# TensorE clears the banks of the sums, and ScalarE fetches a row set in every fourth round

## The chip, the core and the metric

The kernel runs on one core of one Trainium2 chip. Five engines work side by side: TensorE (PE, with its weight loads PEld), VectorE (DVE), ScalarE (ACT), GpSimd (POOL) and SyncE (SP). Each works through its own list of instructions in order and waits on semaphores that others raise. The metric is the device time of one execution in microseconds; less is better.

## The reference

One layer of a graph network with typed edges, then a GRU cell, a residual and a layer norm. There are 12500 nodes of 128 values and 212500 edges, sorted by their target node:

```
all_msgs = einsum('nh,thd->ntd', h, message_W) + message_b        # 8 types
messages = segment_sum(all_msgs[src, edge_type], dst, num_segments=12500)
gi = messages @ gru_w_ih.T + gru_b_ih ;  gh = h @ gru_w_hh.T + gru_b_hh
r = sigmoid(i_r + h_r) ; z = sigmoid(i_z + h_z) ; n = tanh(i_n + r * h_n)
out = layernorm(x + (1 - z) * n + z * h)
```

## The kernel before, in words

The kernel sums rows first and applies the type weights to the sums. The edges lie in tiles of 128, each edge of a tile on a partition. The source rows of a tile are gathered from HBM (128 rows of 512 bytes) by one indirect DMA that GpSimd issues. A product of those rows with a one-hot matrix (made by VectorE) adds them, by target node and type, into one of three PSUM banks `agg[0..2]` ("the sums' banks").

The work goes in 98 rounds, one per tile of 128 nodes. Rounds 0 to 10 ("early") have 17 edge tiles, rounds 11 to 97 ("packed") have 16, in groups c = 0, 1, 2 of 6, 5 and 5 tiles, one bank per group. Round 97 is the last, and has one tile more. In a packed round r:

- GpSimd gathers the 16 tiles of round r into `rows` or `rows_other`, in turn. Before it starts on group c it waits until TensorE has used that group two rounds earlier (`tiles_done`), so it may run nearly two rounds ahead.
- TensorE (`packed_round`) counts, sums group 0, applies the type weights to the sums of round r-1 (`apply_weights`), sums groups 1 and 2, spreads a row of counts of self-loops (`spread_loops`, which needs ScalarE's `copy_loops`), and makes the GRU gates of node tile r-2.
- ScalarE (`packed_round`) does, in this order: the sigmoids of node tile r-3 (`finish_rz`, line 834), a copy, the tanh (`finish_n`, line 842), then `fetch_rows(r, 0)`; then, when group 0 is summed and the weights are applied, it copies `x_turned`, `counts` and `loop_row`, copies bank 0 to SBUF and overwrites the bank with zeros (`copy_sums`, `zero_sums`), the same for bank 1, copies `loops`, does `fetch_rows(r, 1)`, and at last copies and clears bank 2. All these copies stand under line 726.
- VectorE (`packed_round`): one-hot matrices of groups 1 and 2, then `finish(r-3)` (gate arithmetic and layer norm, begun by `t_rh`, line 1238, which needs the sigmoids), masks and a one-hot for round r+1, `add_messages`, `add_loops` (lines 1177 and 1181, which end in the row `work<-work,loop_counts`, and which `copy_loops` on ScalarE waits for), `make_messages`, `loop_x`.

So there is a ring between two engines: sigmoids of round r, VectorE's `finish` to `add_loops`, ScalarE's `copy_loops`, its second batch of `fetch_rows`, its copy of bank 2, and the sigmoids of round r+1.

`fetch_rows` takes one edge tile in six rounds off GpSimd: ScalarE reads row numbers into registers (`TENSOR_LOAD`, line 892) and issues one 512-byte DMA per row (line 896), 16 ahead of the waits of the round and 8 behind `copy_loops`, until 128 rows stand in a spare slot of `rows`. The tile is used as the last of group 2 in rounds 17, 23, ..., 95 (`FETCH_ROUNDS`, 14 of them), where GpSimd gathers 15 tiles in place of 16. SyncE brings the row numbers (`load_fetch_index`).

Of the kernel before, what the change touches and what calls it, by code (L numbers as in the profile page):

```python
# [16 lines left out]
def gnn_kernel(nc, x, src, dst, etype, w_msg, b_msg, w_ih, w_hh, b_ih, b_hh, out):  # L17
# [51 lines left out]
    FETCH_SLOT = (ROUND - 1) % ROW_TILES  # L69
    FETCH_STEP = FETCH_EVERY * ROUND // ROW_TILES  # L70
    FETCH_TILE = GROUPS[2] - 1
    assert FETCH_EVERY * ROUND % ROW_TILES == 0 and (FETCH_EVERY - 1) * (FETCH_AHEAD + FETCH_BEHIND) + FETCH_BEHIND == P
    REACH = (P + SPAN + SAMPLE) // SAMPLE
# [33 lines left out]
    with ctx:  # L107
# [113 lines left out]

        fetch_src = w_ih_rows[:, 0, :].bitcast(I32)
        fetch_index = bias_part[0][0:1, :].bitcast(I32).rearrange("o (s e) -> o s e", e=P)
# [113 lines left out]
        tiles_done = [sem(f"tiles_done{c}") for c in range(3)]  # L337
        sums_read = [sem(f"sums_read{c}") for c in range(3)]
        sums_copied = [sem(f"sums_copied{c}") for c in range(3)]
# [149 lines left out]
        def _(sp):  # L489
# [69 lines left out]
            def load_fetch_index(m):  # L559
                row = (m + 1) * FETCH_STEP + 1  # L560
                sp.dma_start(fetch_index[0:1, m % 2, :], fetch_src[row:row + 1, :]).then_inc(fetch_index_in[m % 2], 16)

# [6 lines left out]
            with sp.If(flag):  # L569
# [25 lines left out]
                for r in range(EARLY + 1, LAST):  # L595
                    round_(r)
                    m = (r - EARLY) // FETCH_EVERY + 1
# [126 lines left out]
        def _(act):  # L724
# [119 lines left out]
            def fields_as_floats(r):  # L844

                for n, name in ((0, "src"), (2, "type"), (3, "next_kind")):
                    act.wait_ge(packing, AT[name])
                    copy(part(n).bitcast(F32)[:, 0:ROW_SLOTS], part(n)[:, 0:ROW_SLOTS]).then_inc(fields_ready, 1)
                    if n == 0:
                        act.wait_ge(fields_ready, 1)  # L850
                        copy(fetch_src[0:ROWS, :], src_words[:, FETCH_SLOT * P:(FETCH_SLOT + 1) * P]).then_inc(fetch_src_ready, 1)

# [30 lines left out]
            def fetch_rows(r, behind):  # L883

                m, step = divmod(r - EARLY - 1, FETCH_EVERY)
                if m >= len(FETCH_ROUNDS) or behind and fetches(r):
                    return
                a = step * (FETCH_AHEAD + FETCH_BEHIND) + behind * FETCH_AHEAD
                n = min(FETCH_BEHIND if behind else FETCH_AHEAD, P - a)
                if step == 0 and not behind:  # L890
                    act.wait_ge(fetch_index_in[m % 2], (m // 2 + 1) * 16)
                _, numbers = nc.values_load_multi_w_load_instructions(
                    fetch_index[0:1, m % 2, a:a + n], engines=[act.engine], min_val=0, max_val=NODES - 1,
                    skip_runtime_bounds_check_because="row numbers, as the gathers take them")
# [659 lines left out]
        def _(pe):  # L1554
# [78 lines left out]
            def sum_tiles(r, c, offs):  # L1633
                _, n, start = groups(r)[c]
                if r > 0:
                    pe.wait_ge(sums_copied[c], r)
                pe.wait_ge(onehot_ready[c], r + 1)
                ahead = isinstance(r, int) and r in (1, 2)
# [5 lines left out]
                for k in range(n):  # L1644
                    if r == LAST:
                        pe.wait_ge(gathered_last[start + k], 16)
                    slot = start + k
                    if fetches(r) and c == 2 and k == FETCH_TILE:
                        m, slot = (r - EARLY) // FETCH_EVERY - 1, SPARE_SLOT
                        pe.wait_ge(fetched[m % 2], (m // 2 + 1) * P * 16)  # L1650
                    last = nc.tensor.matmul(agg[c][:, ds(offs[c][k] * TYPES, CODES)],  # L1651
                                            place[:, slot, :],
                                            onehot[c][:, k, :], start=False, stop=True, skip_group_check=True)
# [235 lines left out]
```

## Time and profile before

| | us |
|---|---|
| three runs | 1990.95, 1994.47, 1996.48 (median 1994.47) |
| the profiled execution, its own time | 1993.74 |
| its span, first to last instruction | 1991.6 |
| mean granted TensorE clock | 0.843 of full speed |

An engine's busy time counts instructions that compute or gather. Issuing a DMA, loading registers and waiting are not counted, so ScalarE's share does not hold the 1792 DMAs of `fetch_rows`. In a timeline, `ACT` rows are computing instructions, `ACTq` rows are DMA issues; the bracket at the end gives the idle time before the row and what ended it. For ScalarE that idle time holds DMA issues too.

### The profile page before, as it was taken

What the parts mean: (1) busy time and instruction counts of PE and PEld (TensorE: products, weight loads), DVE (VectorE), ACT (ScalarE), POOL (GpSimd) and SP (SyncE); (2) the same over time, 40 slices, a digit from 0 to 9 for tenths busy, and PEclk for the clock granted to TensorE, in tenths of its full rate; (3) what the DMA queues carried; (4) which work ended last, traced back from release to release, by engine and by line L of the source; (5) the groups of instructions that cost most, each with busy time, mean ns of one, the idle gap of its engine ahead of it and who ended that gap; (6) DMA issues with size and microseconds to landing.
All of it is one profiled execution on the core that took longest, in us unless ns stands there. A gap on an engine that the chain in (4) does not pass through costs nothing.

```text
span 1991.6 us, 34610 instructions
## 1 busy us (share of the span) xinstructions
PE 1372.3 (69%) x6657; PEld 1045.8 (53%) x6657; DVE 1245.0 (63%) x4650; ACT 595.0 (30%) x1489; POOL 1488.7 (75%) x1578
## 2 busy tenths in 40 slices
PE   1766676767676767676767777767676766766676
PEld 1755555555555555455545555545455555555554
DVE  7887465656565656565656566656565656565566
ACT  2323423232323232323232323232222323232222
POOL 7777777777777777777777777777777777777774
PEclk9877878888888888787878888888888888888889
DMA  5222222222222222222222222222222222222221
GB/s 128 58 62 64 56 64 65 66 62 64 63 66 61 65 63 65 62 65 62 66 61 66 63 65 63 64 63 65 63 64 63 64 63 63 63 65 63 64 63 45
DMA packets 100626, 128.44 MB, mean 64 GB/s; under 512 B 33280, under 2 KB 74959, under 8 KB 100478
## 3 DMA queue, kind: packets, MB, share of 16 engines
q0 software_dynamic: 50112, 102.73, 19.8%
q1 hardware_dynamic: 46584, 23.07, 4.2%
q10 hardware_dynamic: 3782, 0.93, 0.2%
q8 instruction: 61, 1.00, 0.2%
q14 instruction: 87, 0.71, 0.1%
HBM read 120.16 MB, written 6.40 MB: 64 GB/s over the span
## 4 chain that ended last, share of the span: by engine, by line
POOL 65%; issue 22%; DVE 8%; PE 3%; ACT 1%; DMA 1%; DVEq 0%; SPq 0%; ACTq 0%; POOLq 0%
POOL rows_other L660 33%; POOL rows L660 32%; DVE work L1317 1%; DVE codes L1314 1%; PE agg L1651 1%; DVE onehot L1150 1%; PE msg L1678 1%; DMA work<-in_src_dram 0%; DVE root_a L1224 0%; DVE messages_T L1166 0%; ACT sums_room L726 0%; ACT agg L726 0%; DVEq L1157 0%; PE gates L1717 0%; PE turn L1733 0%
## 5 line engine op out<-in xcount | busy, mean ns | idle before, releaser
L660 POOL DMA_INDIRECT rows<-in_x_dram,src_T x843 | 801.2, 950 | 260.9 <-issue 256.1
L660 POOL DMA_INDIRECT rows_other<-in_x_dram,src_T x688 | 651.8, 947 | 209.8 <-issue 209.8
L1651 PE MATMUL agg<-onehot,rows 128*128 128x128 f32 x1714 | 288.0, 330 | 256.9 <-DMA rows<-in_x_dram,src_T 255.9
L1678 PE MATMUL msg<-sums_room,w_type 128*128 128x320 f32 (+1 forms) x1552 | 443.1, 442 | 13.8 <-issue 10.3
L1651 PE MATMUL agg<-onehot,rows_other 128*128 128x128 f32 x1376 | 232.7, 330 | 259.6 <-DMA rows_other<-in_x_dram,src_T 258.3
L1651 PEld LDWEIGHTS agg<-onehot,rows 128*128 128x128 f32 x1714 | 259.6, 236 | 277.6 <-issue 276.6
L1678 PEld LDWEIGHTS msg<-sums_room,w_type 128*128 128x128 f32 x1552 | 306.2, 205 | 122.3 <-issue 27.0
L1199 DVE SCALAR_TENSOR_TENSOR sums_room<-turn,x_turned 128x128 f32<-128x128 f32 x696 | 145.6, 281 | 350.7 <-PE turn L1697 350.7
L1651 PEld LDWEIGHTS agg<-onehot,rows_other 128*128 128x128 f32 x1376 | 208.2, 235 | 278.5 <-issue 278.5
L726 ACT ACTIVATE sums_room<-agg 128x512 f32<-128x512 f32 x293 | 173.3, 591 | 375.7 <-PE agg L1651 327.6
L1150 DVE TENSOR_TENSOR onehot<-code_T,codes 128x640 f32<-128x640 f32 (+1 forms) x294 | 244.3, 859 | 18.9 <-PE agg L1651 18.8
L726 ACT ACTIVATE x_turned<-cnt 128x128 f32<-128x128 f32 x97 | 26.9, 277 | 670.9 <-PE msg L1680 573.9
L726 ACT ACTIVATE agg<-zeros_f 128x512 f32<-128x512 f32 x294 | 176.6, 601 | 9.4
L1138 DVE TENSOR_TENSOR node_mask<-rel_T,codes 128x320 bf16<-128x320 f32 (+3 forms) x294 | 139.1, 473 | 0.0
L1712 PE MATMUL gates<-w_hh_T,x_T 128*128 128x384 f32 x194 | 126.8, 751 | 0.0
L1166 DVE TENSOR_TENSOR messages_T<-messages_T,msg 128x64 f32 x291 | 63.9, 219 | 79.3 <-PE msg L1680 46.8
L1717 PE MATMUL gates<-w_ih_T,messages 128*128 128x384 f32 x194 | 107.5, 646 | 1.9 <-DVE messages L1207 1.9
L1177 DVE TENSOR_TENSOR loop_counts<-counts,loop_row 1x192 f32<-1x192 f32 x87 | 30.4, 350 | 97.1 <-ACT loop_row L726 87.6
L1616 PEld LDWEIGHTS cnt<-node_mask,type_mask 128*128 128x128 bf16 (+1 forms) x783 | 64.4, 105 | 47.6 <-issue 24.7
L1616 PE MATMUL cnt<-node_mask,type_mask 128*128 128x128 bf16 (+1 forms) x783 | 86.9, 228 | 0.0
L1717 PEld LDWEIGHTS gates<-w_ih_T,messages 128*128 128x128 f32 x194 | 54.5, 282 | 51.4 <-issue 42.8
L1181 DVE TENSOR_TENSOR work<-work,loop_counts 1x64 f32 x261 | 56.4, 216 | 37.3 <-DVE loop_counts L1177 0.2
(219 smaller groups left out, 1357.0 us busy)
## 6 DMA issues: line engine op xcount, KB each, us to landing
rows<-in_x_dram ACTq DMA_DIRECT2D x1792, 0.5 KB
rows<-in_x_dram,src_T POOLq DMA_INDIRECT x843, 2.5
rows_other<-in_x_dram,src_T POOLq DMA_INDIRECT x688
x_next<-in_x_dram SPq DMA_DIRECT2D x97, 64.0 KB
out_dram<-out_tile SPq DMA_DIRECT2D x97, 64.0 KB
x_tile<-in_x_dram SPq DMA_DIRECT2D x96, 64.0 KB
work<-in_dst_dram SPq DMA_DIRECT2D x1, 609.4 KB
work<-in_src_dram SPq DMA_DIRECT2D x1, 609.4 KB
```

The lines of the kernel that those rows point to most:

```text
L660: nc.gpsimd.indirect_dma_start(out=to, out_offset=None, in_=x[:, :], in_offset=bass.IndirectOffsetOnAxis(ap=index, axis=0),).then_inc(done ...
L726: return nc.scalar.activation(to, value, ACT.Copy)
L1138: nc.vector.tensor_tensor(node_mask[c][:, 0:n, 0:wide], rel_T[:, cols].unsqueeze(2).broadcast_to([P, n, wide]), codes[:, 0:wide].unsqueeze ...
L1150: nc.vector.tensor_tensor(onehot[c][:, 0:n, :], code_T[:, ds(column(r, start), n)].unsqueeze(2).broadcast_to([P, n, CODES]), codes[:, 0:CO ...
L1166: ins = nc.vector.tensor_tensor(messages_T[:, ds(node, WINDOW)], messages_T[:, ds(node, WINDOW)], bank[:, c * WINDOW:(c + 1) * WINDOW], AL ...
L1181: ins = nc.vector.tensor_tensor(loops_T[:, ds(node, WINDOW)], loops_T[:, ds(node, WINDOW)], (loop_counts if since(r, EARLY) else counts)[0 ...
L1199: done = nc.vector.scalar_tensor_tensor(out=to[:, t, :], in0=turn[:, 0:P], scalar=t - NO_LOOP, in1=values, op0=ALU.is_equal, op1=ALU.mult)
L1616: last = nc.tensor.matmul(cnt[0:m * HALF, c * P:c * P + m * WINDOW], type_mask[c][:, k:k + m, :].rearrange("p k t -> p (k t)"), node_mask[ ...
L1651: last = nc.tensor.matmul(agg[c][:, ds(offs[c][k] * TYPES, CODES)], place[:, slot, :], onehot[c][:, k, :], start=False, stop=True, skip_gr ...
L1678: nc.tensor.matmul(msg[:, 0:cols], w_type[:, t, :], sums[:, t, 0:cols], start=t == 0, stop=False, skip_group_check=True)
L1712: nc.tensor.matmul(bank[:, HID:4 * HID], x_lhs, w_hh_T[:, :], start=False, stop=False)
L1717: nc.tensor.matmul(gates_of(j)[:, 0:GATE], value, w_ih_T[:, :], start=False, stop=True).then_inc(gates_ready, 1)
```

## The change

- `zero_sums` is gone from ScalarE. `copy_sums` raises `sums_copied` by itself. TensorE, in `sum_tiles`, waits for it and clears the bank with a product of zeros (one row of 128 weights by 512 columns, bf16) before it waits for the one-hot and for the gathered rows. This holds for each group of rounds 1 to 97.
- A tile is fetched in every fourth round, in rounds 16, 20, ..., 96 (21 tiles). ScalarE issues 16 row DMAs ahead and 16 behind in each of the rounds 12 to 95, 32 in place of 24 (or 8 in a round that uses a fetched tile).
- The fetched rows land in two places in turn: the spare slot of `rows`, and `w_hh_rows`, whose content is no longer needed.
- The row numbers come from three places of a row of edges and not one; a copy in round 8 is wider for that.

```diff
-    FETCH_EVERY = 6
-    FETCH_AHEAD, FETCH_BEHIND = 16, 8
-    FETCH_ROUNDS = tuple(range(EARLY + FETCH_EVERY, LAST, FETCH_EVERY))
+    FETCH_EVERY = 4
+    FETCH_LOT = 16
+    FETCH_ROUNDS = tuple(range(EARLY + 1 + FETCH_EVERY, LAST, FETCH_EVERY))
+        fetch_rooms = (rows[:, SPARE_SLOT, :], w_hh_rows[:, 0, :])
...
                 read = copy(to, agg[c][:, :].rearrange("p (n t) -> p t n", t=TYPES))
-                if isinstance(r, int) and r == LAST:
-                    read.then_inc(sums_copied[c], 1)
-                else:
-                    read.then_inc(sums_read[c], 1)
-                    act.wait_ge(sums_read[c], r + 1)
-                    zero_sums(c).then_inc(sums_copied[c], 1)
+                read.then_inc(sums_copied[c], 1)
...
                 m, step = divmod(r - EARLY - 1, FETCH_EVERY)
-                if m >= len(FETCH_ROUNDS) or behind and fetches(r):
+                if m >= len(FETCH_ROUNDS):
                     return
-                a = step * (FETCH_AHEAD + FETCH_BEHIND) + behind * FETCH_AHEAD
-                n = min(FETCH_BEHIND if behind else FETCH_AHEAD, P - a)
-                if step == 0 and not behind:
+                a = (2 * step + behind) * FETCH_LOT
+                if a == 0:
                     act.wait_ge(fetch_index_in[m % 2], (m // 2 + 1) * 16)
...
                 for p, number in enumerate(numbers, a):
-                    act.dma_start(rows[p:p + 1, SPARE_SLOT, :], x[ds(number, 1), :]).then_inc(fetched[m % 2], 16)
+                    act.dma_start(fetch_rooms[m % 2][p:p + 1, :], x[ds(number, 1), :]).then_inc(fetched[m % 2], 16)
...
                 if r > 0:
                     pe.wait_ge(sums_copied[c], r)
+                    nc.tensor.matmul(agg[c][:, :], zeros_b[0:1, 0:P], zeros_b[0:1, 0:512], start=True, stop=True)
                 pe.wait_ge(onehot_ready[c], r + 1)
```

The order on ScalarE in the middle of a packed round, before (`x_turned` to the first DMA of the batch behind; an `ISA` row and a `DMA` row together are one fetched row, and 8 such pairs follow in all):

```order
L726 ACTIVATE x_turned<-cnt 128x128
L726 ACTIVATE counts<-cnt 64x192 x2
L726 ACTIVATE loop_row<-cnt 1x192
L726 ACTIVATE sums_room<-agg0 128x8x64
L726 ACTIVATE agg0<-zeros_f 128x512
L726 ACTIVATE sums_room<-agg1 128x8x64
L726 ACTIVATE agg1<-zeros_f 128x512
L726 ACTIVATE loops<-work 1x128
L892 TENSOR_LOAD bias_part0
L896 ISA
L896 DMA rows<-in_x_dram 1x128
```

The same place in the changed kernel, where 16 pairs follow:

```order
L729 ACTIVATE x_turned<-cnt 128x128
L729 ACTIVATE counts<-cnt 64x192 x2
L729 ACTIVATE loop_row<-cnt 1x192
L729 ACTIVATE sums_room<-agg0 128x8x64
L729 ACTIVATE sums_room<-agg1 128x8x64
L729 ACTIVATE loops<-work 1x128
L887 TENSOR_LOAD bias_part0
L891 ISA
L891 DMA w_hh_rows<-in_x_dram 1x128
```

Two clears are gone ahead of `loops`, one more goes behind the copy of bank 2, and the batch between `loops` and that copy is twice as long.

The order on TensorE from the type weights to group 1, before:

```order
L1678 MATMUL msg<-sums_room,w_type 128x320 x8
L1680 MATMUL msg<-counts,b_type 128x192
L1651 MATMUL agg1<-onehot1,rows_other 128x128
L1651 ISA
L1651 MATMUL agg1<-onehot1,rows_other 128x128
```

And in the changed kernel:

```order
L1675 MATMUL msg<-sums_room,w_type 128x320 x8
L1677 MATMUL msg<-counts,b_type 128x192
L1632 MATMUL agg1<-zeros_f 128x512
L1648 MATMUL agg1<-onehot1,rows_other 128x128
L1648 ISA
```

One product of zeros stands ahead of each group, three in a round.

## Rows read from the trace of the kernel before

**Rows 1.** The page's busy time of each engine.
```profile
PE 1372.3 (69%) x6657; PEld 1045.8 (53%) x6657; DVE 1245.0 (63%) x4650; ACT 595.0 (30%) x1489; POOL 1488.7 (75%) x1578
```

**Rows 2.** The page's chain that ended last, by engine.
```profile
POOL 65%; issue 22%; DVE 8%; PE 3%; ACT 1%; DMA 1%; DVEq 0%; SPq 0%; ACTq 0%; POOLq 0%
```

**Rows 3.** Timeline of POOL: start us, us, what; near 1009 us and at the end.
```profile
1008.82 0.95 POOL L660 DMA_INDIRECT rows<-in_x_dram,src_T  x1 [0.30 <-issue]
...
1970.41 0.94 POOL L660 DMA_INDIRECT rows<-in_x_dram,src_T  x1 [0.30 <-issue]
```

**Rows 4.** Timeline of PE in a middle round and near the end.
```profile
1007.94 1.58 PE L1651 MATMUL agg<-onehot,rows 128*128 128x128 f32 x12 [1.93 <-DMA rows<-in_x_dram,src_T]
...
1020.17 2.47 PE L1651 MATMUL agg<-onehot,rows 128*128 128x128 f32 x10 [4.77 <-DMA rows<-in_x_dram,src_T]
...
1953.18 0.28 PE L1697 MATMUL turn<-loops,spread 1*128 1x128 bf16 x1
```

**Rows 5.** Timeline of ACT in a middle round.
```profile
1002.86 0.60 ACT L726 ACTIVATE sums_room<-agg 128x512 f32<-128x512 f32 x1 [4.84 <-PE agg L1651]
...
1005.15 0.26 ACT L834 ACTIVATE gates<-gates 128x128 f32<-128x128 f32 x1 [1.06 <-PE gates L1717]
...
1006.76 0.28 ACT L842 ACTIVATE gates<-t_pre 128x128 f32<-128x128 f32 x1 [0.97 <-DVE t_pre L1240]
1008.12 5.99 ACTq L896 DMA_DIRECT2D rows<-in_x_dram  x16
1014.37 0.28 ACT L726 ACTIVATE x_turned<-cnt 128x128 f32<-128x128 f32 x1 [7.32 <-PE msg L1680]
...
1016.18 0.60 ACT L726 ACTIVATE agg<-zeros_f 128x512 f32<-128x512 f32 x1
1016.72 0.58 ACT L726 ACTIVATE sums_room<-agg 128x512 f32<-128x512 f32 x1
...
1017.86 0.30 ACT L726 ACTIVATE loops<-work 1x128 bf16<-1x128 bf16 x1
1018.74 3.03 ACTq L896 DMA_DIRECT2D rows<-in_x_dram  x8
1022.73 0.60 ACT L726 ACTIVATE sums_room<-agg 128x512 f32<-128x512 f32 x1 [4.57 <-PE agg L1651]
```

**Rows 6.** ACT by line, 280 to 1925 us: busy and mean, idle before, releaser.
```profile
L834 ACT ACTIVATE gates<-gates 128x128 f32<-128x128 f32 x83 | 21.6, 260 | 108.4 <-PE gates L1717 108.2
```

**Rows 7.** Timeline of ACT in round 12.
```profile
275.36 0.26 ACT L834 ACTIVATE gates<-gates 128x128 f32<-128x128 f32 x1 [0.27 <-PE gates L1717]
...
287.75 0.29 ACT L726 ACTIVATE loops<-work 1x128 bf16<-1x128 bf16 x1
288.42 3.03 ACTq L896 DMA_DIRECT2D rows<-in_x_dram  x8
291.57 0.60 ACT L726 ACTIVATE sums_room<-agg 128x512 f32<-128x512 f32 x1 [3.53 <-issue]
...
292.74 0.23 ACT L834 ACTIVATE gates<-gates 128x128 f32<-128x128 f32 x1
```

**Rows 8.** Timeline of DVE in round 12, and in the middle round.
```profile
275.84 0.29 DVE L1238 TENSOR_TENSOR t_rh<-rz,gates 128x128 f32<-128x128 f32 x1
...
286.58 0.92 DVE L1181 TENSOR_TENSOR work<-work,loop_counts 1x64 f32 x3 [0.23 <-DVE loop_counts L1177]
...
1016.84 0.98 DVE L1181 TENSOR_TENSOR work<-work,loop_counts 1x64 f32 x3
```

**Rows 9.** The load of row numbers (line 892): duration in ns, least, median, most.
```profile
L892 ACTq TENSOR_LOAD <-bias_part x154: 713/725/1204, 276.5 to 1920.1; - x154
```

**Rows 10.** Timeline of ACT: the sigmoids of rounds 96 and 97.
```profile
1936.61 0.26 ACT L834 ACTIVATE gates<-gates 128x128 f32<-128x128 f32 x1 [1.43 <-PE gates L1717]
...
1956.54 0.26 ACT L834 ACTIVATE gates<-gates 128x128 f32<-128x128 f32 x1 [1.97 <-PE gates L1717]
```

**Rows 11.** Line 1709: TensorE's products of 128 x 512 in bf16, ns.
```profile
L1709 PE MATMUL gates<-bias_parts,rows x97: 379/606/634, 74.5 to 1975.9; 128*128 128x512 bf16 x97
```

More of the change, by code:

```diff
@@ L65, in gnn_kernel @@
     SAMPLE = 16
-    FETCH_EVERY = 6
-    FETCH_AHEAD, FETCH_BEHIND = 16, 8
-    FETCH_ROUNDS = tuple(range(EARLY + FETCH_EVERY, LAST, FETCH_EVERY))
-    FETCH_SLOT = (ROUND - 1) % ROW_TILES
-    FETCH_STEP = FETCH_EVERY * ROUND // ROW_TILES
+    FETCH_EVERY = 4
+    FETCH_LOT = 16
+    FETCH_ROUNDS = tuple(range(EARLY + 1 + FETCH_EVERY, LAST, FETCH_EVERY))
+    FETCH_PLACES = tuple(divmod((r - EARLY) * ROUND + ROUND - 1, ROW_TILES) for r in FETCH_ROUNDS)
+    FETCH_SLOTS = 3
     FETCH_TILE = GROUPS[2] - 1
-    assert FETCH_EVERY * ROUND % ROW_TILES == 0 and (FETCH_EVERY - 1) * (FETCH_AHEAD + FETCH_BEHIND) + FETCH_BEHIND == P
+    FETCH_FIRST = min(slot for _, slot in FETCH_PLACES)
+    assert FETCH_EVERY * 2 * FETCH_LOT == P
+    assert all((slot - FETCH_FIRST) % FETCH_EVERY == 0 for _, slot in FETCH_PLACES) and FETCH_SLOTS * FETCH_EVERY == ROW_TILES
     REACH = (P + SPAN + SAMPLE) // SAMPLE
@@ L195, in gnn_kernel @@
         zeros_f = sb("zeros_f", [P, 512])
+        zeros_b = zeros_f[:, :].bitcast(BF16)
         messages_T = sb("messages_T", [P, ACC_ROWS])
@@ L219, in gnn_kernel @@
         assert TYPES * END_COLS + P + HID <= (EARLY + 4) * P
-        fetch_src = w_ih_rows[:, 0, :].bitcast(I32)
+        fetch_src = w_ih_rows[:, :, :].rearrange("p a e -> p (a e)").bitcast(I32).rearrange("p (a e) -> p a e", e=P)
+        fetch_rooms = (rows[:, SPARE_SLOT, :], w_hh_rows[:, 0, :])
         fetch_index = bias_part[0][0:1, :].bitcast(I32).rearrange("o (s e) -> o s e", e=P)
@@ L337, in gnn_kernel @@
         tiles_done = [sem(f"tiles_done{c}") for c in range(3)]
-        sums_read = [sem(f"sums_read{c}") for c in range(3)]
         sums_copied = [sem(f"sums_copied{c}") for c in range(3)]
@@ L559, in load_fetch_index @@
             def load_fetch_index(m):
-                row = (m + 1) * FETCH_STEP + 1
-                sp.dma_start(fetch_index[0:1, m % 2, :], fetch_src[row:row + 1, :]).then_inc(fetch_index_in[m % 2], 16)
+                row, slot = FETCH_PLACES[m]
+                sp.dma_start(fetch_index[0:1, m % 2, :], fetch_src[row:row + 1, (slot - FETCH_FIRST) // FETCH_EVERY, :]).then_inc(fetch_index_in[m % 2], 16)
             def round_(r):
@@ L596, in _ @@
                     round_(r)
-                    m = (r - EARLY) // FETCH_EVERY + 1
+                    m = (r - EARLY - 2) // FETCH_EVERY + 1
                     if fetches(r - 1) and m < len(FETCH_ROUNDS):
@@ L764, in _ @@
             copy(w_hh_T[:, :], msg[:, 0:GATE]).then_inc(turned_copied, 1)
-            def zero_sums(c):
-                return copy(agg[c][:, :], zeros_f[:, :])
             def zero_counts():
@@ L850, in fields_as_floats @@
                         act.wait_ge(fields_ready, 1)
-                        copy(fetch_src[0:ROWS, :], src_words[:, FETCH_SLOT * P:(FETCH_SLOT + 1) * P]).then_inc(fetch_src_ready, 1)
+                        slots = src_words[:, 0:ROW_SLOTS].rearrange("r (a k e) -> r a k e", k=FETCH_EVERY, e=P)
+                        copy(fetch_src[0:ROWS, :, :], slots[:, :, FETCH_FIRST, :]).then_inc(fetch_src_ready, 1)
             def copy_field(n):
@@ L885, in fetch_rows @@
                 m, step = divmod(r - EARLY - 1, FETCH_EVERY)
-                if m >= len(FETCH_ROUNDS) or behind and fetches(r):
+                if m >= len(FETCH_ROUNDS):
                     return
-                a = step * (FETCH_AHEAD + FETCH_BEHIND) + behind * FETCH_AHEAD
-                n = min(FETCH_BEHIND if behind else FETCH_AHEAD, P - a)
-                if step == 0 and not behind:
+                a = (2 * step + behind) * FETCH_LOT
+                if a == 0:
                     act.wait_ge(fetch_index_in[m % 2], (m // 2 + 1) * 16)
                 _, numbers = nc.values_load_multi_w_load_instructions(
-                    fetch_index[0:1, m % 2, a:a + n], engines=[act.engine], min_val=0, max_val=NODES - 1,
+                    fetch_index[0:1, m % 2, a:a + FETCH_LOT], engines=[act.engine], min_val=0, max_val=NODES - 1,
                     skip_runtime_bounds_check_because="row numbers, as the gathers take them")
                 for p, number in enumerate(numbers, a):
-                    act.dma_start(rows[p:p + 1, SPARE_SLOT, :], x[ds(number, 1), :]).then_inc(fetched[m % 2], 16)
+                    act.dma_start(fetch_rooms[m % 2][p:p + 1, :], x[ds(number, 1), :]).then_inc(fetched[m % 2], 16)
             def packed_round(r):
@@ L1646, in sum_tiles @@
                         pe.wait_ge(gathered_last[start + k], 16)
-                    slot = start + k
+                    tile_rows = place[:, start + k, :]
                     if fetches(r) and c == 2 and k == FETCH_TILE:
-                        m, slot = (r - EARLY) // FETCH_EVERY - 1, SPARE_SLOT
+                        m = (r - EARLY - 1) // FETCH_EVERY - 1
+                        tile_rows = fetch_rooms[m % 2]
                         pe.wait_ge(fetched[m % 2], (m // 2 + 1) * P * 16)
                     last = nc.tensor.matmul(agg[c][:, ds(offs[c][k] * TYPES, CODES)],
-                                            place[:, slot, :],
+                                            tile_rows,
                                             onehot[c][:, k, :], start=False, stop=True, skip_group_check=True)
```

## The prediction

> **What bounds the kernel now.** I read the busy shares first: POOL has the most, 75%, and ACT only 30% [rows 1]. The chain that ended last is POOL for 65% and "issue" for 22%, which together is nearly all of the span [rows 2]. The POOL timeline shows why: each gather takes 0.95 us and 0.30 us of issue lies before it, so one starts every 1.25 us, from the start to 1970.41 [rows 3]. TensorE waits for the gathers, 1.93 us before group 0 and 4.77 us before group 2 of a round [rows 4]. So by the page, GpSimd is the bound, and a gather taken from it is worth 1.25 us.
>
> The second reading is ScalarE's timeline, since its 30% leaves out the DMA issues [rows 5]. In the middle round, which lasts 19.87 us (1002.86 to 1022.73), 16 row DMAs take 5.99 us and 8 take 3.03, so 0.37 us for each one after the first, and ScalarE can do nothing else meanwhile. What is free is 1.06 us before the sigmoids, 0.97 before the tanh and 0.96 before the copy of bank 2 (1021.77, where the batch ends, to 1022.73). The mean wait at the sigmoids is 108.4 / 83 = 1.3 us [rows 6]. That is the slack of the ring that runs through ScalarE and VectorE.
>
> **How fast the ring is when nothing else holds it.** The trace shows this once: in round 12, after a late start, the sigmoids begin at 275.36 and the next at 292.74, 17.38 us later, with 24 DMAs between [rows 7]. GpSimd's pace is 20.0 us for 16 gathers, so the ring had over 2 us to spare. I take it apart:
>
> - Sigmoids to VectorE's last `add_loops`: 275.36 to 287.50 (286.58 + 0.92) is 12.14 us [rows 7, 8]. VectorE started on `t_rh` 0.48 us after the sigmoids and was never idle for long.
> - From there to the first DMA of the batch behind: 288.42 - 287.50 = 0.92. In the middle round it is 1018.74 - 1017.82 = 0.92 too [rows 5, 8], although the copy of `loops` starts 0.25 us after VectorE's end in one and 0.04 in the other. So the loading of row numbers hangs on VectorE's end.
> - The batch of 8: 3.03. To the copy of bank 2: 0.12. That copy with its clear to the next sigmoids: 1.17.
> - Sum 12.14 + 0.92 + 3.03 + 0.12 + 1.17 = 17.38.
>
> **The change part by part.**
>
> *Seven gathers fewer.* 21 fetched tiles for 14: 7 x 1.25 = 8.75 us off GpSimd. A round then has 15.75 gathers in the mean, 19.7 us.
>
> *Three clears off ScalarE.* The two ahead of `loops` (0.60 each, 1016.18 for one) give the ring nothing: what comes next waits for VectorE at 1017.82, and VectorE's work between the sigmoids and that point is untouched. The third, behind the copy of bank 2, is on the ring: 1.17 becomes 0.54, the pitch from such an operation to the next (1016.18 to 1016.72). In the early rounds, where ScalarE and TensorE answer each other, the clears may give up to 1 us once; I take 0.
>
> *Eight more DMAs behind `loops`.* 3.03 becomes 5.99, as in the batch ahead. The load of 16 numbers takes 1.20 us against 0.72 for 8 [rows 9]; the batch ahead shows it too, 1006.76 to 1008.12 is 1.36 where 8 numbers need 0.88 (1017.86 to 1018.74). So 0.92 becomes 1.40.
>
> *The ring after:* 12.14 + 1.40 + 5.99 + 0.12 + 0.54 = 20.19 us. From below: a round without the 0.23 us pause in VectorE's row [rows 8], 19.96, say 20.0. From above: a batch of 16 that takes 0.29 us longer, as one batch in four does before, and somewhat more for longer code, 20.35. I take 20.17. That is over the 19.7 that GpSimd needs. **The ring becomes the bound by 0.47 us a round**, in each of the 84 rounds that fetch (12 to 95).
>
> The batch of `fetch_rows` ahead of the waits is not what decides: from the sigmoids to the tanh 1.6 us (of which VectorE's share is less when it is free), 7.35 to the end of the DMAs, 0.26 to `x_turned` at 1014.37 and 1.2 to the end of `loop_row` (the clear at 1016.18 less one copy of 0.6) make 10.4 at most, and VectorE needs that row only 10.64 after the sigmoids (286.58 less the pause of 0.23 and one operation of 0.35, less 275.36).
>
> *Three products of zeros on TensorE.* A 128 x 512 product in bf16 took 0.38 to 0.61 us [rows 11]; three are 1.1 to 1.8 us a round. Two stand ahead of a wait for gathers of 1.93 and 4.77 us, the one of group 1 eats into the second of these [rows 4]. Covered, and more so when the ring is late. If not covered, they would cost GpSimd nothing until TensorE is nearly two rounds behind. At the very end the one for group 2 of round 97 stands on the path: 0.3 us.
>
> *Two places for the rows, index loads, wider copy.* The rows land a round before use, the copy is in round 8 beside waits: 0.
>
> *What waits behind the late ring.* When ScalarE is late, TensorE's `apply_weights` starts late, but it had 4 us before that and 4.8 before group 2. GpSimd's gathers run nearly two rounds ahead and would be held only when the ring is about 30 us late or more (an estimate: gathers for round r+2 begin some 1.7 rounds of 20 us after the sigmoids of round r). So the lateness grows quietly, 0.47 x 84 = 39 us, and is paid at the end.
>
> **The sum.** Rounds 12 to 96 are 84 rings from the sigmoids at 275.36: 275.36 + 84 x 20.17 = 1969.6, where before the same sigmoids stood at 1936.61 [rows 10], held by GpSimd. Round 96 fetches nothing: VectorE 12.1, copy of `loops` 0.3, then from `spread_loops` to the sigmoids 3.4 (1953.18 to 1956.54) [rows 4, 10] make 15.8 in place of 19.93; at full clock it may be 15. I take 15.4: 1985.0. The rest, 1991.6 - 1956.54 = 35.1, is a chain of latencies of the last two node tiles and stays, with 0.3 for the product: span 2020.4. Around the span lie 1993.74 - 1991.6 = 2.1: 2022.5. The rings' own bounds give 84 x (20.0 to 20.35) = 2008 to 2038. Since GpSimd may be caught up with late and the lower bound 20.0 is the sum of undisturbed rows, I name 2020, which is a ring of 20.14. The profiled execution lies 0.7 us below the median of the runs; that is inside their spread.
>
> **Rules of the Trainium skill.** ScalarE's DMA issue is shown above as 0.37 us per row, 5.99 for 16. "DMA: Bandwidth & Descriptors", section "Issuing engines are not separate DMA queues", says that issuing from another engine saves the sequencer's time for it, "which is usually small relative to the DMA itself". Read so, the 896 extra issues are near to free, and the kernel ends where rival 1 does. The trace does not agree for 512-byte rows: 32 issues are 12 us of a 20 us round. Of the number load, "Perfetto Trace Analysis", section "DVE / Act Engine Instruction", says that an instruction that waits is pushed to a wait queue and the sequencer is ready for the next. By that the load could be done before VectorE ends (rival 2). The constant 0.92 us of this trace speaks against it.
>
> **Rivals.**
>
> 1. *GpSimd stays the bound.* The ring turns out at 19.7 or less, and only the seven gathers count: 1993.74 - 8.75 + 0.3 = 1985.3. For it: the page's chain, ScalarE's 30%, 2 us of waits in its round. Against: those waits plus the freed 0.63 are 3.6, but the 0.97 is VectorE's own time and the addition is 3.4. It decides when the ring is under 19.7; at 19.86 the lateness is (19.86 - 19.7) x 84 = 13 us, of which round 96 gives back 4, and gain and loss cancel.
> 2. *The number load starts before VectorE ends*, once ScalarE has two clears fewer ahead of it. The ring loses up to 1.2 us: 19.0, and the time is that of rival 1, 1985. Against: both rounds above.
> 3. *The ring is only just over.* 19.8 to 19.95: lateness 8 to 21 us, less 4, on 1985: 1989 to 2002, no change in the middle.
> 4. *Row DMAs slow the gathers.* At 1008.82, inside a batch, a gather takes 0.95 as elsewhere [rows 3]. 1% on 1558 gathers would be 15 us beside rival 1, 2000. Little speaks for it.
>
> **Chances.** The forecast 0.79, rivals 1 and 2 together 0.12, rival 3 0.07, rival 4 0.02. About 0.3% (6 us) is what a measurement of this kernel tells from no change. Slower: the forecast and some of rivals 3 and 4, 0.82; same 0.06; faster 0.12. The range reaches from rival 3's end, 2001, to a ring of 20.32, 2035; below it lies the 0.12 of rivals 1 and 2 and a little of 3.
>
> **What would show it.** Right: POOL loses its place at the head of the chain that ended last, to ACTq, ACT and DVE; the distance between two rows of the sigmoids is 20.1 in the middle of the run, whatever the number of gathers; their wait for PE gates is gone; the copy of bank 2 comes right behind a batch of 6.0 us; the first DMA of that batch 1.40 us after VectorE's `work` row; GpSimd's gathers keep 1.25 us and end some 30 us earlier against the end of the span than the 21 us of now. Wrong: sigmoids every 19.7 us with waits before them (rival 1), a first DMA under 1 us after VectorE (rival 2), or gathers over 0.95 us (rival 4).

## The result, and the profile after

| | before | changed |
|---|---|---|
| median (runs) | 1994.01 (1990.95 to 1996.48, 4) | 2029.97 (2027.0 to 2030.8, 4) |
| profiled execution, its span | 1993.74, 1991.6 | 2029.68, 2027.7 |
| mean granted clock | 0.843 | 0.853 |

The ratio is 1.018, with a 95% interval of 1.0168 to 1.0193: 1.8% slower. The forecast was 2020 (2001 to 2035).

The page of the changed kernel, busy time of the engines (beside [rows 1]) and the chain that ended last (beside [rows 2]):

```profile
PE 1446.3 (71%) x6852; PEld 1033.3 (51%) x6948; DVE 1248.3 (62%) x4650; ACT 417.7 (21%) x1198; POOL 1483.0 (73%) x1571
```

```profile
DVE 36%; ACTq 23%; issue 19%; DVEq 11%; ACT 6%; PE 3%; DMA 0%; SPq 0%
```

Every engine's share is within 9 points of before, and POOL still has the most. The chain is another one: POOL had 65% of it and is gone; VectorE, ScalarE's issues and ScalarE have taken its place.

ScalarE's timeline in a middle round (start us, us, what; the bracket is the idle time before the row, in which DMA issues are counted as idle), beside [rows 5]:

```profile
1006.11 0.27 ACT L829 ACTIVATE gates<-gates 128x128 f32<-128x128 f32 x1
...
1007.25 0.28 ACT L837 ACTIVATE gates<-t_pre 128x128 f32<-128x128 f32 x1 [0.48 <-DVE t_pre L1235]
1008.61 5.99 ACTq L891 DMA_DIRECT2D w_hh_rows<-in_x_dram  x16
1014.85 0.28 ACT L729 ACTIVATE x_turned<-cnt 128x128 f32<-128x128 f32 x1 [7.32 <-issue]
...
1015.69 0.32 ACT L729 ACTIVATE loop_row<-cnt 1x192 f32<-1x192 f32 x1
...
1018.25 0.31 ACT L729 ACTIVATE loops<-work 1x128 bf16<-1x128 bf16 x1 [1.13 <-DVE work L1176]
1019.61 6.27 ACTq L891 DMA_DIRECT2D w_hh_rows<-in_x_dram  x16
1026.00 0.60 ACT L729 ACTIVATE sums_room<-agg 128x512 f32<-128x512 f32 x1 [7.45 <-issue]
1026.50 0.27 ACT L829 ACTIVATE gates<-gates 128x128 f32<-128x128 f32 x1
```

The copy of bank 2 and the sigmoids follow the batch without a wait; before, they waited for TensorE. VectorE's timeline in the same round, beside [rows 8]:

```profile
1006.61 0.29 DVE L1233 TENSOR_TENSOR t_rh<-rz,gates 128x128 f32<-128x128 f32 x1 [4.86 <-ACT rz L830]
...
1016.76 0.34 DVE L1172 TENSOR_TENSOR loop_counts<-counts,loop_row 1x192 f32<-1x192 f32 x1 [1.12 <-ACT loop_row L729]
1017.25 0.97 DVE L1176 TENSOR_TENSOR work<-work,loop_counts 1x64 f32 x3
```

VectorE now stands idle 4.86 us ahead of `t_rh` and waits for the sigmoids. The bracket of `loop_counts` names ScalarE's `loop_row`, but that row was done at 1016.01, 0.75 us earlier. What fills the 1.12 us is seen in the chain that ended last, whose longest pieces there are (start us, us, what):

```profile
1015.54 0.31 DVEq L1152
1015.99 0.30 DVEq L1152
1016.41 0.30 DVEq L1152
1016.76 0.35 DVE loop_counts L1172
```

Line 1152 is `first_nodes`: VectorE loads three node numbers into registers, which no busy time counts. They lie on the ring, and in the mean of 84 rings the idle time ahead of `loop_counts` is 1.12 us as well. By line, 280 to 1925 us (busy and mean ns, idle before, releaser), beside [rows 6]:

```profile
L1233 DVE TENSOR_TENSOR t_rh<-rz,gates 128x128 f32<-128x128 f32 x81 | 23.3, 288 | 381.1 <-ACT rz L830 381.1
L829 ACT ACTIVATE gates<-gates 128x128 f32<-128x128 f32 x81 | 22.1, 273 | 0.0
```

The sigmoids' 108.4 us of waiting are 0.0, and VectorE's waiting for them is 381.1. GpSimd's timeline in the same round and at the end, beside [rows 3]:

```profile
1006.71 0.94 POOL L663 DMA_INDIRECT rows<-in_x_dram,src_T  x1 [0.30 <-issue]
...
1974.21 0.94 POOL L663 DMA_INDIRECT rows<-in_x_dram,src_T  x1 [0.30 <-issue]
1985.09 0.94 POOL L663 DMA_INDIRECT rows<-in_x_dram,src_T  x1 [9.93 <-PE agg L1648]
```

A gather is as long as before. From 1336 us on GpSimd waits for TensorE once in a while, 23 times and 31.4 us in all, of which 9.93 stand ahead of the very last gather, which waits for TensorE's round 96; the one ahead of that ends 52.6 us before the end of the span, where the last one of before ended 20.2 us before it. The sigmoids of rounds 96 and 97, beside [rows 10]:

```profile
1976.50 0.27 ACT L829 ACTIVATE gates<-gates 128x128 f32<-128x128 f32 x1
...
1992.38 0.26 ACT L829 ACTIVATE gates<-gates 128x128 f32<-128x128 f32 x1 [3.00 <-PE gates L1714]
```

### The profile page after: what moved, and what is told of

Read it like the earlier page. It is cut to its first block, busy times and chain, and to the rows that moved or that the text cites. A ratio compares the mean times of both kernels' runs of the same rounds, so it can differ in the third digit from the quotient of the medians.

```text
span 2027.7 us, 37507 instructions
## 1 busy us (share of the span) xinstructions
PE 1446.3 (71%) x6852; PEld 1033.3 (51%) x6948; DVE 1248.3 (62%) x4650; ACT 417.7 (21%) x1198; POOL 1483.0 (73%) x1571
## 3 DMA queue, kind: packets, MB, share of 16 engines
q10 hardware_dynamic: 5574, 1.39, 0.3%
## 4 chain that ended last, share of the span: by engine, by line
DVE 36%; ACTq 23%; issue 19%; DVEq 11%; ACT 6%; PE 3%; DMA 0%; SPq 0%
ACTq L891 19%; DVEq L1152 8%; ACTq L887 4%; DVE root_a L1219 3%; DVE work L1176 3%; DVE messages_T L1161 3%; DVE rstd L1221 2%; DVE type_mask L1136 2%; DVE loop_counts L1172 2%; DVE stats L1254 1%; DVE t_pre L1235 1%; DVE t_y L1252 1%; DVE gates L1250 1%; DVE t_d L1246 1%; DVE t_zd L1248 1%
## 5 line engine op out<-in xcount | busy, mean ns | idle before, releaser
L663 POOL DMA_INDIRECT rows_other<-in_x_dram,src_T x667 | 631.9, 947 | 207.0 <-issue 197.9
L1233 DVE TENSOR_TENSOR t_rh<-rz,gates 128x128 f32<-128x128 f32 x97 | 27.9, 288 | 408.5 <-ACT rz L830 406.5
L1648 PE MATMUL agg<-onehot,rows 128*128 128x128 f32 x1736 | 264.8, 306 | 11.3 <-DMA rows<-in_x_dram,src_T 11.3
L1694 PE MATMUL turn<-loops,spread 1*128 1x128 bf16 x88 | 23.7, 269 | 347.4 <-ACT loops L729 347.0
L1648 PEld LDWEIGHTS agg<-onehot,rows 128*128 128x128 f32 x1736 | 232.0, 211 | 51.7 <-issue 51.6
L1648 PE MATMUL agg<-onehot,rows_other 128*128 128x128 f32 x1334 | 195.1, 297 | 0.0
L1648 PEld LDWEIGHTS agg<-onehot,rows_other 128*128 128x128 f32 x1334 | 169.6, 203 | 31.6 <-issue 31.6
L1714 PE MATMUL gates<-w_ih_T,messages 128*128 128x384 f32 x194 | 135.6, 800 | 0.9 <-DVE messages L1202 0.9
L1632 PE MATMUL agg<-zeros_f 1*128 1x512 bf16 x291 | 119.3, 410 | 0.0
L1611 PE MATMUL cnt<-node_mask,type_mask 128*128 128x128 bf16 (+1 forms) x783 | 109.0, 269 | 0.0
```

The source lines that it names most:

```text
L663: nc.gpsimd.indirect_dma_start(out=to, out_offset=None, in_=x[:, :], in_offset=bass.IndirectOffsetOnAxis(ap=index, axis=0),).then_inc(done ...
L1611: last = nc.tensor.matmul(cnt[0:m * HALF, c * P:c * P + m * WINDOW], type_mask[c][:, k:k + m, :].rearrange("p k t -> p (k t)"), node_mask[ ...
L1714: nc.tensor.matmul(gates_of(j)[:, 0:GATE], value, w_ih_T[:, :], start=False, stop=True).then_inc(gates_ready, 1)
```

## The experiments

Two theories. *Ring*: the ring of ScalarE and VectorE (sigmoids, `finish` to `add_loops`, `copy_loops`, the batch behind, copy of bank 2, sigmoids) sets the pace, because 8 more row DMAs stand on it. *Rival*: something else does, namely TensorE's products of zeros, the gathers, or the mere total of ScalarE's or a queue's work, wherever it stands.

Twelve kernels ran in four sets. One circumstance has to be known for the numbers: each set ran on a chip of its own, and only the last on one where the kernel before takes 1994 us, as it did above. In the other three it takes 2447 to 2479 us. "Slower chip" below means a chip of these three sets; as each was used in one set only, the runs can't tell a property of the chip from one of the hour. Each kernel is held against the kernel before on its own chip, and each trace is read for its own bounds. Even these ratios carry over only roughly: one and the same program (18 and 14 rows) has 1.077 in one set and 1.089 in another.

| kernel | this | before there | ratio (95%) |
|---|---|---|---|
| e1_clear_only | 2466.1 | 2479.4 | 0.9946 (0.9926 to 0.9965) |
| e2_fetch_only | 2731.9 | 2479.4 | 1.1021 (1.0998 to 1.1043) |
| e3_18_14 | 2668.7 | 2479.4 | 1.0766 (1.0745 to 1.0787) |
| e4_newton1 | 2683.3 | 2479.4 | 1.0822 (1.0800 to 1.0844) |
| f0_changed | 2665.2 | 2446.9 | 1.0899 (1.0870 to 1.0929) |
| f1_clear_only | 2435.5 | 2446.9 | 0.9953 (0.9935 to 0.9970) |
| f3_18_14 | 2660.7 | 2446.9 | 1.0885 (1.0852 to 1.0917) |
| f6_numbers_early | 2646.7 | 2446.9 | 1.0819 (1.0782 to 1.0857) |
| s0_before_const | 2406.7 | 2451.6 | 0.9815 (0.9785 to 0.9846) |
| s1_const | 2425.6 | 2451.6 | 0.9895 (0.9866 to 0.9924) |
| s2_const_18_14 | 2407.8 | 2451.6 | 0.9816 (0.9787 to 0.9846) |
| g0_no_rows | 2010.6 | 1993.8 | 1.0090 (1.0073 to 1.0107) |

### No row DMAs at all (g0_no_rows)

```diff
         def fetches(r):
-            return isinstance(r, int) and r in FETCH_ROUNDS
+            return False
...
-                if m >= len(FETCH_ROUNDS):
+                if True:
                     return
```

> The changed kernel without any row fetched by ScalarE: GpSimd gathers all 16 tiles of every round, and TensorE clears the banks as in the changed kernel. It tells whether ScalarE's row DMAs, and the waits inside them, are what holds the kernels on a chip where the kernel before takes about 2450 us. Theory: without them the ring has 6 us or more to spare and GpSimd bounds at 16 x 1.25 = 20.0 us a round in every round; on such a chip the sigmoids of round 12 stand at 380 us, 84 rounds of 20.0 are 1680, and the end is 50 us behind: 2110 to 2135 us, so GpSimd's 35 gathers more cost nothing against 300 us of the row DMAs. Where the kernel before takes 1994 us: 1985 + 21 x 1.25 = 2011 us. Rival (these chips are slow in other engines as well, the row DMAs are only one part): 2300 us or more.

This is the run that tells the theories apart, and it fell on a chip with the time of the result. It took 2010.6 us against 2011 by the GpSimd sum. GpSimd issues 21 gathers more than in the changed kernel, and the whole is 19 us *faster* than it (ratios to the kernel before 1.009 and 1.018, with intervals that don't touch, and medians of the kernel before that are 0.2 us apart). The page's chain of this kernel:

```profile
POOL 65%; issue 22%; DVE 8%; PE 3%; ACT 1%; DMA 0%; DVEq 0%; SPq 0%; ACTq 0%; POOLq 0%
```

These are the shares of before, to a point. The same two lines as above, 280 to 1925 us:

```profile
L1233 DVE TENSOR_TENSOR t_rh<-rz,gates 128x128 f32<-128x128 f32 x82 | 23.4, 285 | 11.2 <-ACT rz L830 9.8 <-ACT gates L829 1.2
L829 ACT ACTIVATE gates<-gates 128x128 f32<-128x128 f32 x82 | 21.5, 262 | 176.6 <-PE gates L1714 176.6
```

The sigmoids wait 176.6 us for TensorE, and VectorE hardly waits for them: the ring is slack. Its own length without rows can be read in round 12, from ScalarE's timeline:

```profile
277.33 0.26 ACT L829 ACTIVATE gates<-gates 128x128 f32<-128x128 f32 x1 [0.91 <-PE gates L1714]
...
289.54 0.31 ACT L729 ACTIVATE loops<-work 1x128 bf16<-1x128 bf16 x1 [2.43 <-DVE work L1176]
289.75 0.57 ACT L729 ACTIVATE sums_room<-agg 128x512 f32<-128x512 f32 x1
291.77 0.26 ACT L829 ACTIVATE gates<-gates 128x128 f32<-128x128 f32 x1 [1.45 <-PE gates L1714]
```

It is 291.77 - 277.33 = 14.44 us, in which the sigmoids wait 1.45 us for TensorE's gates; the 12.21 from the sigmoids to the copy of `loops` are the changed kernel's 12.14. Put the batch in (from the copy of `loops` to that of bank 2 it takes 7.47 in a round of 5.99 us of DMAs, in place of 0.21) and take off the wait that it covers (from that copy to the sigmoids 0.49 in place of 2.02): 14.44 + 7.26 - 1.53 = 20.17, the changed kernel's ring within 0.1. So the changed kernel passes from GpSimd's bound to the ring's by the row DMAs alone, and products of zeros, which this kernel has too, are not what costs. Before plus 14 gathers of 1.25 us would be 1993.8 + 17.5 = 2011.3; measured are 2010.6, and the interval is some 3 us either way, so nothing that can be told from zero is left for them.

This run takes the rows away altogether, so it does not by itself tell their place from their total. For the place there is the trace of the changed kernel above: the chain that ended last goes through its middle round by VectorE and ScalarE alone, and in that round ScalarE stands idle for 1.13 us ahead of `loops` and waits for VectorE (1.01 in the mean of 84). If ScalarE's total were the bound, it would not.

### The two halves of the change (e1 and f1: clears only; e2: fetching only)

Clears only is the kernel before with this, and without `zero_sums`:

```diff
                     pe.wait_ge(sums_copied[c], r)
+                    nc.tensor.matmul(agg[c][:, :], zeros_b[0:1, 0:P], zeros_b[0:1, 0:512], start=True, stop=True)
```

> The kernel before with one part of the change alone: TensorE clears the banks, ScalarE does not; the fetching stays one tile in six rounds. Theory (the ring through ScalarE and VectorE is what got slow, by the longer batch behind `loops`): the ring here is 17.4 - 0.6 = 16.8 us when free, GpSimd stays the bound, 1991 to 1996 us, no change. Rival (the products of zeros on TensorE cost the time, 291 of 0.41 us = 119 us busy, and an early part that starts the packed rounds 2.8 us later): slower, 2005 us or more.

> The kernel before with the products of zeros on TensorE in place of ScalarE's clears, and the fetching as before. Where the kernel before takes 1994 us, the theory that GpSimd bounds it expects 1991 to 1996 us: the ring gets 0.6 us shorter and has slack anyway, and TensorE's three products are covered by its waits for gathers. If TensorE's products delay the gathers or the start of the packed rounds: 1997 to 2005. Where the ring bounds the kernel before (2479 us), it was 2466.

Fetching only is the changed kernel with ScalarE's clears in place of that product:

> The changed kernel with the clears back on ScalarE: 32 rows fetched a round, no product of zeros. Theory: the ring is 20.22 us as measured plus 0.63 for the one clear that lies on it, 20.85; the two clears ahead of `loops` hide in VectorE's time. 84 rings are 53 us more than in the changed kernel: 2080 us (2070 to 2088). Rival 1 (all three clears are on the ring, 1.8 us): 2180. Rival 2 (the products of zeros are the cost): near the kernel before, 1985 to 1995.

On two chips clears only is 0.5% faster than before, and fetching only, on the first of them, is 10.2% slower. So the loss goes with the fetching and not with the products of zeros; the sizes of the expectations were missed by far, since they were worked out for a chip on which GpSimd bounds the kernel before. Here the clears-only form has a ring of 24.09 us (e1) and 23.74 (f1), where GpSimd needs 20.0 at most, and no GpSimd in the chain that ended last. The kernel before left no trace on such a chip; that it is bound in the same way there is inferred. Fetching only (ring 27.30 us, mean of 84) against the changed kernel (26.55, on another of the slower chips) gives 0.75 us a ring for the clears that are off ScalarE, 0.1 of which may be the chips' (the program with 18 and 14 rows takes 8 us more on the first). The time from the copy of bank 2 to the sigmoids, which I had at 1.17 to 0.54, is 1.16 against 0.49 in the means of these two traces.

### The changed kernel, and rows or work moved within the ring (f0, e3 and f3, f6, e4)

18 rows ahead and 14 behind (e3, f3):

```diff
+    FETCH_AHEAD = 18
-                a = (2 * step + behind) * FETCH_LOT
+                a = 2 * step * FETCH_LOT + behind * FETCH_AHEAD
+                n = 2 * FETCH_LOT - FETCH_AHEAD if behind else FETCH_AHEAD
```

Numbers early (f6) calls `copy_loops(r)` inside `fetch_rows(r, 1)`, between the load of the numbers and the first DMA. e4 leaves out two of the three steps of the root's iteration in layer norm:

```diff
-NEWTON = 3
+NEWTON = 1
```

> The changed kernel itself, as the base that the other kernels of this set are compared with on the same chip. Where the kernel before takes about 1994 us: 2030 us. Where it takes about 2479 us, with gaps in ScalarE's row DMAs, the ring theory expects it well above the kernel before, since 8 more DMAs and a longer load of numbers stand on the ring: the fetch-only kernel took 2732 there, and without its clear on the ring it should be 84 x 0.6 to 84 x 1.2 us less, 2630 to 2690; the rival that GpSimd bounds expects it at or below the kernel before.

> The changed kernel with the 32 rows of a round cut 18 ahead and 14 behind, and not 16 and 16. Theory: behind `loops` the ring loses 2 rows of 0.37 + 0.06 us, 0.86; ahead of it the batch takes 0.86 more, of which VectorE's own 10.64 us hide 0.6. The ring is 19.6, just under GpSimd's 19.7, so GpSimd is the bound again and the seven gathers count: 1985 to 1990 us. Rival (the number of DMAs that ScalarE issues in a round is what costs, wherever they stand): 2030, as the changed kernel.

> The changed kernel with 18 of a round's 32 row DMAs ahead of the waits and 14 behind loops, in place of 16 and 16; nothing else. Ring theory: two DMAs less on the ring are 0.74 us and the shorter load of numbers 0.1, so 20.22 becomes 19.4, GpSimd's 19.7 is the bound again, and the time is 1985 to 1992 us where the changed kernel takes 2030. On a chip where the ring stays the bound, 84 x 0.84 = 70 us less than the changed kernel, more where the DMAs have gaps. Rival (the total of ScalarE's or the queue's work counts, not its place): no change, since 32 DMAs are issued either way. If the batch ahead now ends too late for loop_row, part of the 0.84 is lost: 2000 to 2010.

> The changed kernel with the load of the second batch's 16 row numbers ahead of the copy of loops in place of behind it, so it can be done while ScalarE waits for VectorE. Ring theory: the time from VectorE's last add_loops to the first DMA falls from 1.40 us to about 0.4 (the copy of loops is 0.3), the ring from 20.22 to 19.2 to 19.3, and GpSimd bounds: 1985 to 1992 us. On a chip where the ring stays the bound: 84 x 0.9 = 75 us less than the changed kernel. Rival (the load doesn't lie on the ring, or waits for something else): 2030, no change.

> The changed kernel with 1 step of the root iteration in place of 3, so the norm's root is rough; VectorE's `finish` gets four small operations shorter, about 0.9 us. Theory: VectorE lies on the ring, which becomes 0.6 us shorter (then ScalarE's own batch ahead holds `loop_row`): 19.6, and GpSimd is the bound: 1985 to 1990. Rival (ScalarE alone is full, VectorE is not on the ring): no change, 2030.

The changed kernel came as expected, and none of the others did: f3 gained 4.5 us in place of 70, with runs that overlap those of f0, f6 gained 18.5 in place of 75, and e4 takes 14.6 us longer than e3 in the same set, where both were to end at one time. The reason stands in the traces. ScalarE's timeline of f0_changed:

```profile
1311.38 0.27 ACT L829 ACTIVATE gates<-gates 128x128 f32<-128x128 f32 x1
...
1323.91 0.31 ACT L729 ACTIVATE loops<-work 1x128 bf16<-1x128 bf16 x1 [0.42 <-issue]
1325.26 12.64 ACTq L891 DMA_DIRECT2D rows<-in_x_dram  x16
1338.03 0.60 ACT L729 ACTIVATE sums_room<-agg 128x512 f32<-128x512 f32 x1 [13.81 <-issue]
1338.52 0.27 ACT L829 ACTIVATE gates<-gates 128x128 f32<-128x128 f32 x1
```

The same 16 DMAs take 12.64 us where they took 5.99. Line 891 by operation (duration in ns, least, median, most), first in the kernel of the result, then in f0_changed:

```profile
L891 ACTq FUSED_REGOPS  x2688: 37/37/37, 280.4 to 1975.5; - x192
L891 ACTq DMA_DIRECT2D rows<-in_x_dram x1408: 213/213/490, 280.5 to 1975.7; - x176
```

```profile
L891 ACTq FUSED_REGOPS  x2688: 2/37/730, 380.0 to 2607.4; - x192
L891 ACTq DMA_DIRECT2D rows<-in_x_dram x1408: 3/213/717, 380.2 to 2607.6; - x176
```

The medians are equal. But on this chip there are stretches in which one instruction of ScalarE starts 0.7 us after the other, whatever it does: here an address computation of 37 ns takes up to 730. The mean parts of the 84 rings from the sigmoids of round 12 to those of 96, in us, from these traces:

| | sigmoids to `loops` | `loops` to first DMA | batch behind | to sigmoids | ring |
|---|---|---|---|---|---|
| changed, the result's chip | 12.14 | 1.35 | 6.10 | 0.62 | 20.22 |
| f0_changed | 12.45 | 1.36 | 12.13 | 0.62 | 26.55 |
| f3_18_14 | 13.45 | 3.38 | 9.10 | 0.62 | 26.55 |
| f6_numbers_early | 12.60 | 0.13 | 12.98 | 0.62 | 26.34 |
| e4_newton1 | 12.40 | 1.36 | 12.39 | 0.62 | 26.77 |

What f3 takes from the batch behind comes back in the batch ahead and in the pause before the first DMA; what f6 takes from the load comes back in the batch. And e4 makes VectorE's work shorter (busy 11.3 us a ring for 12.0) without bringing `loops` earlier. In f0, f3, f6 and e4 VectorE's `loop_counts` starts 0.03 to 0.06 us after the end of ScalarE's `loop_row` in the mean, where there are 0.66 on the result's chip: the batch ahead has become part of the ring. So these traces show that ScalarE's own row of instructions bounds the kernel on such a chip. They don't test whether 18 and 14 rows bring it back under GpSimd's pace on the other kind. On this kind the rival "the total counts, not its place" fits f3 (a ring of 26.55 us in both orders).

### Constant row numbers (s0, s1, s2)

One instruction for a DMA in place of three (an address computation, a move, the issue), and half as many DMAs again to keep a batch at 6 us:

```diff
-                    act.dma_start(fetch_rooms[m % 2][p:p + 1, :], x[ds(number, 1), :]).then_inc(fetched[m % 2], 16)
+                    cut = HID // 2 if p % 2 else HID
+                    act.dma_start(fetch_rooms[m % 2][p:p + 1, 0:cut], x[p:p + 1, 0:cut]).then_inc(fetched[m % 2], 16)
+                    if p % 2:
+                        act.dma_start(fetch_rooms[m % 2][p:p + 1, cut:HID], x[p:p + 1, cut:HID]).then_inc(fetched_parts[m % 2], 16)
```

> The kernel before, but its row DMAs read rows with constant numbers (0 to 127), so an issue is one instruction of ScalarE in place of three, and every second row goes as two halves: 24 DMAs ahead and 12 behind in place of 16 and 8; the load of the numbers stays. It leaves out that the rows are the edges' own. Theory of the instruction supply: the stretches of 0.7 us from one instruction of ScalarE to the next come from too many instructions and are gone, the batch of 12 takes about 3 us, GpSimd bounds as it does where the kernel before takes 1994 us, and the time is 1990 to 2010 us. Rival (the DMA queue can't take more rows, so the issues wait): as slow as the kernel before on the same chip, or slower, since there are half as many DMAs again.

> The changed kernel with constant row numbers (0 to 127) and every second row in two halves: 24 DMAs in each batch, one instruction each. It leaves out that the rows are the edges' own. Ring theory: with no stretches of waiting for instructions, sigmoids to the copy of loops 12.1 to 12.5 us, 1.4 to the first DMA, the batch behind B as measured (about 6 us), and 0.6 to the next sigmoids: the ring is 14.2 + B, about 20.2 us, over GpSimd's 19.7, and the time 2015 to 2035 us, slower than the kernel before in the same form. Rival (GpSimd or the total of the DMAs bounds): a ring of 19.7, 1985 to 1992 us. Rival (the queue): as slow as the changed kernel on the same chip or slower.

> As the changed kernel with constant row numbers and halves, but 18 of a round's 32 rows ahead of the waits and 14 behind loops: 27 and 21 DMAs in place of 24 and 24. Ring theory: three DMAs less behind loops are worth 3 x 0.25 us and the load of 14 numbers 0.1, so the ring is 19.4 by itself and GpSimd's 19.7 bounds: 1985 to 1992 us, 30 to 45 us less than with 24 and 24, though the number of DMAs is the same. Rival (the total of ScalarE's work counts, not its place): the same time as with 24 and 24.

The times are 2407 to 2426, not 1990 to 2035: the stretches did not go. The issues in s1_const, the whole rows and first halves:

```profile
L893 ACTq DMA_DIRECT2D rows<-in_x_dram x1408: 3/265/778, 379.4 to 2366.8; - x176
```

ScalarE has 6182 instructions in place of 10384 while half as many DMAs again go to the queue, and the ring is 23.68 us in place of 26.55. That speaks against a queue that can't take more rows. But a batch of 24 behind takes 9.77 us in the mean where the median of the batches ahead is 7.0, so with 40% fewer instructions the stretches are rarer and not gone. What starts one stays open. By its measured parts the ring of s1 is 13.52 + 0.01 + 9.77 + 0.39 = 23.7. It takes 19 us more than s0 on the same chip; the direction is the expected one, at another bound. In s2 the batch behind is down to 6.21 us, yet `loops` comes 17.04 after the sigmoids, since the batch ahead takes 10.94 (the first DMAs of the batch behind start 0.36 us ahead of that copy in the mean): a ring of 17.04 - 0.36 + 6.21 + 0.61 = 23.50, and 18 us less time. As above, such a chip says nothing on GpSimd's bound.

## Why the prediction was right

**The bound changes hands.** As predicted. The ring's mean is (1976.50 - 278.19) / 84 = 20.22 us, GpSimd's pace by its gathers is 15.75 x 1.25 = 19.7, and g0_no_rows shows GpSimd's bound coming back when the row DMAs go.

**The ring's parts.** Medians of those 84 rings but the first: sigmoids to the copy of `loops` 12.14, from there to the first DMA 1.36 (in the middle round 1019.61 - 1018.22 = 1.39 from VectorE's end, forecast 1.40), the batch 5.99, to the copy of bank 2 0.12, to the sigmoids 0.49. The sum is 20.11. I had 20.19 from these parts and went down to 20.14. The mean is over the median because 33 of 83 batches behind take 6.27 us in place of 5.99; "one in four" was too few. My reason for going down, that GpSimd may be caught up with late, was none: the sigmoids never waited.

The 12.14 us of VectorE hold more than the prediction read in them. "Never idle for long" passes over the 1.12 us of register loads ahead of `loop_counts`, in each ring of the kernel before as of the changed one. That the batch ahead is not what decides was right: in the middle round `loop_row` is done 9.90 us after the sigmoids (forecast at most 10.4), and VectorE takes it at 10.65. And the issuing time was set against the length of a round, not against a row's own transfer, of which no view here gives the length.

**The sum, term by term:**

| term | forecast | measured | difference |
|---|---|---|---|
| sigmoids of round 12 | 275.36 | 278.19 | +2.8 |
| 84 rings | 84 x 20.14 = 1691.8 | 1698.3 | +6.5 |
| round 96 | 15.4 | 15.88 | +0.5 |
| tail, with the last product | 35.4 | 35.32 | -0.1 |
| around the span | 2.1 | 1.98 | -0.1 |
| sum | 2020.1 | 2029.7 | +9.6 |

The mechanism was right and two sizes were off. Round 96 was 12.1 + 3.8; the 15.8 worked out from rows was right and the 15.4 that I took was not.

**The clears in the early rounds** I had at 0, with a gain of up to 1 us. The start is 2.8 us later, and in g0_no_rows, which fetches nothing, round 12's sigmoids stand at 277.33, 2.0 later. So, as far as one trace of each can tell, about 2.0 go with the clears on TensorE, and 0.9 are left to the rest. In g0_no_rows it costs nothing at the end, since GpSimd's gathers, which bound it, run a little *ahead* there: its last one starts at 1985.08, and 1970.41 + 14 x 1.25 = 1987.9. In the changed kernel, bound by the ring, it is paid.

**The products of zeros** are covered elsewhere, as predicted. Their line on the page of the changed kernel:

```profile
L1632 PE MATMUL agg<-zeros_f 1*128 1x512 bf16 x291 | 119.3, 410 | 0.0
```

That is 1.2 us a round, in the lower part of the forecast's 1.1 to 1.8, while TensorE waits for `loops` alone 347.0 us in all, 4 us a round:

```profile
L1694 PE MATMUL turn<-loops,spread 1*128 1x128 bf16 x88 | 23.7, 269 | 347.4 <-ACT loops L729 347.0 <-DVE sums_room L1194 0.4
```

**The clear off ScalarE** was priced at 0.63 a ring; on the slower chips 0.67 is read in that place. **GpSimd held late:** its first wait for TensorE in a packed round is at 1336 us, when the ring is some 52 x 0.52 = 27 us behind GpSimd's pace (forecast: about 30). **Rival 2**, the early load of numbers, did not happen: 1.39 us from VectorE's end to the first DMA, none under 1. **Rival 4**: the gathers are 951 and 947 ns in the mean, as before. **Rival 1** (1985) is what the gathers alone would give: 2010.6 - 21 x 1.25 = 1984.4. The 46 us between that and the result are the ring.

**Not settled.** A kernel with a shorter batch behind, or the numbers loaded early, is by the parts above under GpSimd's pace (20.11 less 0.74 and 0.1 is 19.3, and the 0.66 us between `loop_row` and `loop_counts` would take most of the two rows that move there). So, just, is one in which VectorE's three register loads stand earlier, beside other work, as those ahead of `messages_T` do in this trace without any idle time: `loop_counts` could then follow `loop_row` at once, 20.22 less 0.6. These are estimates; no such kernel ran on a chip where GpSimd bounds. No version has beaten both kernels on such a chip. On the slower ones clears only did, by 0.5%.

## What to carry to other kernels

An engine's busy share holds neither its DMA issues nor its register loads, so before work is moved to an engine that looks idle, follow its row for one round and add up the ring through it: here ScalarE showed 30% and had 2.6 us to spare of 20. Best is a round in which nothing else holds the ring, such as the first one after a late start: its length, plus what is added, against the present bound's pace gives the time. And leave a margin: a change that moves the bound from one engine to another by half a microsecond a round loses over 84 rounds more than it won.

## What the runs showed of the hardware that was not expected

The kernel before takes 1994 us in the set of the result and in the last one, and 2447 to 2479 on three other chips. Gathers (0.95 us) and single DMA issues (213 ns in the median) are the same on both. On the slower ones there are stretches in which each instruction of ScalarE starts 0.7 us after the one before, and they make the batch of 16 row DMAs behind `loops` 12.1 us in the mean in place of 6.1. The row DMAs are not all of it, nor is ScalarE: the sigmoids of round 12 stand at 378 us in place of 278, and no row is fetched by then. TensorE has such stretches there, in which a weight load and a product take 1.4 us together (f0_changed, timeline of PE in an early round):

```profile
98.47 0.37 PE L1648 MATMUL agg<-onehot,kinds_T 128*128 128x128 f32 x1 [1.04 <-issue]
99.87 0.37 PE L1648 MATMUL agg<-onehot,kinds_T 128*128 128x128 f32 x1 [1.03 <-issue]
101.27 0.37 PE L1648 MATMUL agg<-onehot,kinds_T 128*128 128x128 f32 x1 [1.03 <-issue]
```

The mean granted clock is lower there too, 0.792 in f0_changed for 0.853. The changed kernel, which is 1.8% slower on one kind, is 9.0% slower on the other. What the cause of the difference is, no run shows.
